# Attention over 16 batches on one core: x transposed by TensorE in every body, the projection's bias written by VectorE, other buffer rings

## The reference

```python
qkv = (x @ w_qkv).reshape(b, n, 3, H, hd).transpose(2, 0, 3, 1, 4)
q, k, v = (qkv[0], qkv[1], qkv[2])
attn = jnp.einsum('bhnd,bhmd->bhnm', q, k) * scale
attn = jnp.where(attn_mask[None, None] == 0, -jnp.inf, attn)
attn = jax.nn.softmax(attn, axis=-1)
o = jnp.einsum('bhnm,bhmd->bhnd', attn, v).transpose(0, 2, 1, 3).reshape(b, n, d)
o = o @ w_proj + b_proj
...
return o + ln                      # ln: layer norm of o, with gamma and beta
...
x = _layernorm(x + _L0_gnn_ref(x, ...), axis=-1)
```

## Time and profile before

| | |
|---|---|
| median of 3 runs | 3227.46 us (3222.18 to 3236.81) |
| the profiled execution | 3231.68 us, of which the span is 3229.8 us |
| PE busy | 2994.3 us, 93% of the span |
| POOL, ACT, DVE busy | 2628.1, 2624.1, 2197.0 us |
| mean granted clock of PE | 0.973 of full speed |

### The profile page before, as it was taken

One profiled execution on the slowest core, in us unless ns is written; L12 is line 12 of the kernel. 1 busy time (PEld: TensorE's weight loads), 2 busy tenths in 40 slices (PEclk: granted clock), 3 DMA queues, 4 the chain that ended last, 5 costly groups with the idle time before them and its releaser, 6 DMA issues.

```text
span 3229.8 us, 119607 instructions
## 1 busy us (share of the span) xinstructions
PE 2994.3 (93%) x42112; PEld 1842.0 (57%) x42112; DVE 2197.0 (68%) x4243; ACT 2624.1 (81%) x3790; POOL 2628.1 (81%) x1610
## 2 busy tenths in 40 slices
PE   5889999899998999999999998999999899999995
PEld 2556556565565556656566565556556566565562
DVE  4546667677676767767677676767767677676775
ACT  5878878788787878878788787888888788787882
POOL 4768878788787878878798797888878788787884
PEclk9989999999999999999999999999999999999997
DMA  8999999999999999999999999999999999999994
GB/s 225 192 199 195 211 214 218 218 208 220 211 212 218 215 214 219 216 212 219 214 216 214 215 213 222 216 215 220 216 214 219 212 212 219 212 215 218 216 208 108
DMA packets 2320778, 682.49 MB, mean 211 GB/s; under 512 B 2268498, under 2 KB 2268498, under 8 KB 2320724
## 3 DMA queue, kind: packets, MB, share of 16 engines
q1 hardware_dynamic: 2266724, 581.58, 97.3%
q10 hardware_dynamic: 54000, 100.16, 9.7%
HBM read 77.60 MB, written 33.55 MB: 34 GB/s over the span
## 4 chain that ended last, share of the span: by engine, by line
POOL 54%; issue 29%; SPq 7%; PE 6%; DMA 2%; DVE 1%; POOLq 1%; ACT 1%; ACTq 0%; DVEq 0%
POOL p_split L742 42%; SPq L307 5%; POOL x_res L758 4%; POOL x_split L776 4%; POOL norm L766 2%; POOL norm L761 2%; PE scores_a L401 1%; PE side L360 1%; SPq L285 1%; DMA pt<-p_split 1%; PE side L347 1%; POOL shift L769 1%; POOLq L741 1%; PE proj L383 0%; PE pv_bank L422 0%
## 5 line engine op out<-in xcount | busy, mean ns | idle before, releaser
L742 POOL TENSOR_TENSOR p_split<-p,p_split 128x1024 f16<-128x1024 f32 x1024 | 2172.4, 2138 | 531.8 <-ACT p_split L507 526.0
L494 ACT ACTIVATE p<-p,row_min 128x1024 f32<-128x1024 f32 x1024 | 1167.9, 1142 | 91.9 <-DVE row_min L638 89.8
L507 ACT ACTIVATE p_split<-p 128x1024 f16<-128x1024 f32 x1024 | 1053.6, 1046 | 206.8 <-DMA pt<-p_split 205.9
L638 DVE CUSTOM_DVE_ANT_0 p<-scores_a,mask_q 128x1024 f32<-128x1024 f32 x512 | 626.9, 1224 | 502.3 <-PE scores_b L401 481.9
L422 PE MATMUL pv_bank<-v_both,pt 128*128 128x64 f16 x8192 | 840.0, 195 | 26.5 <-DMA pt<-p_split 24.6
L424 PE MATMUL pv_bank<-v_both,pt 128*128 128x64 f16 x8192 | 840.6, 195 | 0.0
L423 PE MATMUL pv_bank<-v_both,pt 128*128 128x64 f16 x8192 | 840.5, 195 | 0.0
L422 PEld LDWEIGHTS pv_bank<-v_both,pt 128*128 128x128 f16 x8192 | 747.9, 99 | 115.2 <-issue 39.6
L360 PE MATMUL side<-xt,w_hi 128*128 128x512 f16 x2048 | 683.2, 391 | 119.3 <-DMA xt<-x_split 114.3
L423 PEld LDWEIGHTS pv_bank<-v_both,pt 128*128 128x128 f16 x8192 | 736.9, 99 | 84.4 <-issue 6.0
L424 PEld LDWEIGHTS pv_bank<-v_both,pt 128*128 128x128 f16 x8192 | 737.4, 99 | 0.0
(11 more groups left out here) (80 smaller groups left out, 4261.3 us busy)
## 6 DMA issues: line engine op xcount, KB each, us to landing
x_in<-in_x ACTq DMA_DIRECT2D x63, 512.0 KB, 5.1
x_res<-in_x ACTq DMA_DIRECT2D x120, 256.0 KB, 3.3
out<-x_res ACTq DMA_DIRECT2D x120, 256.0 KB, 3.7
pt<-p_split SPq DMA_TRANSPOSE x1024, 4.8
pt<-in_adj SPq DMA_DIRECT2D x8, 512.0 KB, 9.7
ot<-in_L_gnn_w_qkv SPq DMA_DIRECT2D x4, 768.0 KB, 9.8
p<-in_x SPq DMA_DIRECT2D x4, 512.0 KB, 5.3
p<-in_x ACTq DMA_DIRECT2D x8, 256.0 KB, 8.5
```

The source lines that it names most:

```text
L494: nc.scalar.activation(p32[:, slot, :], p32[:, slot, :], ACT.Exp, bias=row_min[:, slot:slot + 1], scale=-1.0, accum_out=row_sum[:, head:he ...
L507: nc.scalar.activation(p_split[:, head % RING, HI, :], p32[:, head % RING, :], ACT.Copy).then_inc(hi_done, 1)
L638: nc.vector.tensor_tensor_reduce(out=p32[:, slot, :], in0=scores[ab][:, :], in1=mask_q[:, u, :], scale=-SCALE, scalar=3.0e38, op0=ALU.add, ...
L742: nc.gpsimd.tensor_tensor(p_split[:, slot, LO, :], p32[:, slot, :], p_split[:, slot, HI, :], ALU.subtract).then_inc(lo_done, 1)
```

## The change

X becomes a side item. `X0` and `X1` are four float32 transposes each by PE of the two tiles in `x_in`, into a side bank; ACT takes the high part into `xt` and DVE the low one, as it takes any other side item. This happens in every body but the last batch's, so `xt` is held twice, addressed by the batch's parity, and `x_split`, the DMA transposes of x and the splits of x on ACT and POOL are gone, with the waits of Q0 and K1 for them. The first batch's x is transposed the same way ahead of body -1. The bias is written by DVE: after each last read of the projection's bank a `seed` puts 256 times the bias into it, and the twelve products accumulate on it; P0 and P1 have twelve items, the `ones` product is gone, and P waits for its seed where it waited for the last read. `p_split` becomes a ring of eight (`SPLIT`), `pt` one of four (`TURNED`). The loop covers bodies 5 to 58. Slots of takes move: Q1 is taken at slots 3 and 4.

```diff
 RING = 4
-TURNED = 8
+TURNED = 4
+SPLIT = 8
...
-ORDER = [("Q1", 0, 12), ("V0", 0, 48), ("V1", 0, 48), ("P0", 0, 4), ("O1", 0, 4), ("P0", 4, 13), ("Q0", 0, 12),
-         ("K0", 0, 12), ("K1", 0, 12), ("P1", 0, 9), ("O0", 0, 4), ("P1", 9, 13)]
+ORDER = [("Q1", 0, 12), ("X0", 0, 4), ("V0", 0, 48), ("V1", 0, 48), ("P0", 0, 4), ("O1", 0, 4), ("P0", 4, 7),
+         ("X1", 0, 4), ("P0", 7, 12), ("Q0", 0, 12), ("K0", 0, 12), ("K1", 0, 12), ("P1", 0, 9), ("O0", 0, 4),
+         ("P1", 9, 12)]
...
-LOOP = (PAIRS + 1, GROUPS - 1)
+LOOP = (PAIRS + 1, GROUPS - PAIRS - 1)
...
-TAKE_DVE = {"Q1": 6, "V0": 10, "V1": 12, "O1": 14, "Q0": 22, "K0": 29, "K1": 29, "O0": 30}
+TAKE_DVE = {"Q1": 4, "X0": 5, "V0": 10, "V1": 11, "O1": 14, "X1": 15, "Q0": 22, "K0": 29, "K1": 30, "O0": 30}
...
-        x_split = sb("x_split", [P, T // 2, 2, 2, D], F16)
-        xt = sb("xt", [P, T, 2, KC, P], F16)
+        xt = sb("xt", [P, 2, T, 2, KC, P], F16)
...
-                for u in range(UNITS):
-                    for p in range(T // 2):
-                        if u == XT_UNIT[p] and not (known(g) and g == FIRST_GROUP):
-                            transposing(sp, g, lambda: turn_x(g, p))
...
+                elif kind[0] == "X":
+                    if i == 0 and half == 0:
+                        wait_alone(pe, x_in_loaded, g * 16 + 16)
+                    mm = nc.tensor.transpose(bank[:, i * P:(i + 1) * P], x_in[:, half, i * P:(i + 1) * P], ident[:, :])
...
-                    mm = nc.tensor.matmul(bank[:, c * P:(c + 1) * P], xt[:, t, rows, k, :], w[:, k, OF_V, pair(g), :],
+                    mm = nc.tensor.matmul(bank[:, c * P:(c + 1) * P], xt[:, parity(batch(g)), t, rows, k, :],
+                                          w[:, k, OF_V, pair(g), :],
                                           start=(i == 0), stop=(i % 12 == 11), skip_group_check=True)
...
-                    if i == 0 and kind == NEXT_FIRST:
-                        wait_alone(pe, x_turned[0], batch(g + 1) * 32 + 32)
-                    if i == 0 and kind == "K1":
-                        wait_alone(pe, x_turned[1], batch(g + 1) * 32 + 32)
+                    if i == 0 and kind == NEXT_FIRST and active(g, "X1"):
+                        wait_alone(pe, side_dve, side_done(g, "X1"))
...
-                else:
-                    nc.tensor.matmul(proj_bank(g, half), ones[:, :], bias_rows[:, :], start=False, stop=True).then_inc(proj_ready, 1)
...
+                elif kind[0] == "X":
+                    nc.scalar.activation(xt[:, parity(batch(g + PAIRS)), pair(g) * 2 + half, HI, :, :],
+                                         bank[:, :].rearrange("p (k n) -> p k n", k=KC), ACT.Copy).then_inc(side_act, 1)
...
-                before = unit_before(ug, uk, RING // 2)
+                before = unit_before(ug, uk, SPLIT // 2)
                 if not known(before[0]) or before[0] >= 0:
-                    wait(act, turned[(head - RING) % TURNED], turned_before(before[0], before[1], ab) + 16)
+                    wait(act, turned[(head - SPLIT) % TURNED], turned_before(before[0], before[1], ab) + 16)
...
+            def seed(g, i):
+
+                nc.vector.tensor_scalar(proj_bank(g, i), bias_b[:, :], WSCALE, None, ALU.mult).then_inc(seeds(g, i)[0], 1)
...
                     nc.vector.scalar_tensor_tensor(xr, bank, norm[:, i:i + 1], xr, ALU.mult, ALU.add).then_inc(summed, 1)
+                    wait_alone(dve, summed, n + 1)
+                    if not known(g) or g < GROUPS - 1:
+                        seed(g + i, 1 - i)
...
-            def split(g):
-                if known(g) and not 0 <= batch(g) < B - 1:
-                    return
-                wait_alone(pool, x_hi_done, g + PAIRS + 1)
-                nc.gpsimd.tensor_tensor(x_split[:, pair(g), :, LO, :], x_in[:, :, :], x_split[:, pair(g), :, HI, :],
-                                        ALU.subtract).then_inc(x_lo_done, 1)
```

More of the change, by code:

```diff
@@ L233, in bodies @@
                 body(g)
-        def transposing(eng, g, do):
-            if not known(g):
-                with eng.If((g & 3) == 3):
-                    do()
-            elif (g + 1) % PAIRS == 0 and 0 <= batch(g + 1) < B:
-                do()
         def heads(g, u, ab):
@@ L257, in proj_bank, with seeds @@
             return scores[0][:, 0:CH] if known(g) and g >= GROUPS and i == 1 else proj[:, :]
+        def seeds(g, i):
+            if known(g) and g >= GROUPS:
+                return (seeded[0], projected(GROUPS, 0) + (g - GROUPS + 1)) if i == 0 else (seeded[1], g - GROUPS + 1)
+            return seeded[0], projected(g, i) + 1
         def last_tile(g, i):
@@ L272, in _ @@
         def _(sp):
-            for t in range(T // 2):
-                sp.dma_start(x_first[:, t, :, :], x_pairs[t, :, :, :]).then_inc(x_first_loaded[t], 16)
+            for t in range(T):
+                sp.dma_start(x_first[:, t, :], x_tiles[t, :, :]).then_inc(x_first_loaded[t], 16)
             for kc in range(KC):
@@ L327, in _, with first_turn @@
             pe.wait_ge(ident_ready, 1)
+            def first_turn(t):
+                pe.wait_ge(x_first_loaded[t], 16)
+                wait(pe, x_first_lo, t - 1)
+                for k in range(KC):
+                    mm = nc.tensor.transpose(side[t % 2][:, k * P:(k + 1) * P], x_first[:, t, k * P:(k + 1) * P], ident[:, :])
+                mm.then_inc(x_first_turned, 1)
             def side_matmul(g, kind, i):
@@ L370, in project @@
                         pe.wait_ge(w_ready, 4 * KC)
-                        pe.wait_ge(bias_ready, 4)
-                    if known(g) and g >= GROUPS:
-                        pe.wait_ge(min_done, heads(GROUPS, 0, 0))
-                        pe.wait_ge(summed, projected(g, half) - (1 if g > GROUPS or half else 0))
-                    else:
-                        wait_alone(pe, summed, projected(g, half))
+                    wait_alone(pe, *seeds(g, half))
                     if half == 0:
@@ L425, in times_v @@
                 mm.then_inc(pv_done, 1)
+            for t in range(T):
+                first_turn(t)
+            for k in range(KC):
+                mm = nc.tensor.matmul(proj[:, k * P:(k + 1) * P], ident[:, :], ident[:, :], start=(k == 0), stop=True,
+                                      skip_group_check=True)
+            mm.then_inc(bits_set, 1)
             def body(g):
@@ L619, in take @@
                                             ot[:, HI, parity(batch(og)), pair(og), tiles, :], ALU.subtract).then_inc(side_dve, 1)
+                elif kind[0] == "X":
+                    at, tile = parity(batch(g + PAIRS)), pair(g) * 2 + half
+                    nc.vector.tensor_tensor(xt[:, at, tile, LO, :, :], bank[:, :].rearrange("p (k n) -> p k n", k=KC),
+                                            xt[:, at, tile, HI, :, :], ALU.subtract).then_inc(side_dve, 1)
                 elif kind[0] == "V":
@@ L715, in body @@
                     if known(g) and g == FIRST_GROUP and s == 0:
-                        prepare_weights()
+                        for t in range(T):
+                            first_low(t)
+                            if t % 2:
+                                prepare_weights(t // 2)
                         for t in range(T):
```

152 lines of the change are left out of this document (64 added, 88 removed).

## The result

The changed kernel takes 3246.1 us (median of 7 runs, 3243.4 to 3253.8), the kernel before in the same series 3229.9; the ratio is 1.005, with a 95% interval from 1.0038 to 1.0061. It is slower by a half per cent, where a gain of one per cent was forecast; the time lies inside the wide range of 3130 to 3250, at its upper end. The profiled execution took 3243.4 us, its span 3241.6.

What follows compares the result with a forecast made beforehand. PE, busy 93% of the span, bounds the kernel. Loop body 46.06 - 0.29 - 0.43 + 0.93 + 2.1, taken as 48.35; the bodies' -29.5 with start and end makes -31.5, median 3196 us, range 3130 to 3250.

Steps and rivals of the forecast that it cites:

- the term for register instructions and the lost lead: V in loop bodies: 1.3 us for register instructions plus 0.7 for the lost lead, 2.0 in replay, 2.1 in the sum.
- V0's wait for Q1's low part: Ahead of V0: ends 1.1 to 1.5 us into unit 1's products, nearly spends the sequencer's lead, costs 0.7 us.
- the transposes: X0 and X1 on PE: eight at a step of 0.12 us add 0.93 us a body.
- Break-even: Loop body at which the total would not change: 48.93 us.
- Rival (b): V0's wait ends later than 1.9 us into unit 1, lead spent throughout; body 49.5, total 3258; chance 0.13.
- The stall for x: Long bodies, ahead of Q0: the whole excess of 9.2 us goes, 15 x 9.2 = 139 us.
- The bias: Two bias products a body leave PE: -0.43 us.
- O0's gap: Transposes of O0 waiting for K0's low part: the gap of 0.3 us in a short body goes, -0.29.
- rival (d): TURNED = 4 or X's takes delay times_v by 0.5 to 0.8 us a body: 3223 to 3239; chance 0.1.
- rival (c): Transposes of x cost their printed length or slow the clock: +1.3 us a body, 3274; chance 0.03.
- Rival (a): V's register instructions hide as their printed length says: loop body 46.3 to 46.5, total 3091; chance 0.11.
- being written out: Bodies outside the loop have fixed addresses: 46.3 us each, four of them behind the loop.

Runs made afterwards that it cites:

- before_reg: The kernel before with V's tile of xt in the loop indexed by a register that always holds zero: 3279.7 us, ratio 1.0155.
- x_after_v: The changed kernel with X0 moved from ahead of V0 to behind O1, so V0 doesn't wait for Q1's low part: 3414.5 us, ratio 1.0568.
- rings_old: The changed kernel with the old rings, four heads of split probabilities and eight of transposed ones: 3246.2 us, ratio 1.0044.
- x_first: The changed kernel with X0 ahead of Q1, so V0 waits for X0's take instead: 3213.4 us, ratio 0.9940.
- x_first63: x_first with the loop to body 62, no wait of Q0 for X1, and second-tile scaling two slots later: 3195.9 us, ratio 0.9898.
- mix_late: x_first63 with 24 V0 products dealt among Q1's last four and X0 taken a slot earlier on ACT: 3178.7 us, ratio 0.9832.
- branch: x_first without Q0's wait for X1, and units 1 and 2 written twice on PE behind a branch on batch parity: 3824.8 us, ratio 1.1833.
- loop8: The changed kernel with eight bodies in the loop, run six times, making pair and parity constants: 3365.0 us, ratio 1.0417.
- xv: x_first without Q0's wait, scaling two slots later, V reading a third x copy filled by DMA each batch, four-head rings: 3276.7 us, ratio 1.0140.

## Why the prediction was wrong

**The step that failed** is the size of the term for register instructions and the lost lead: 2.1 us a body in the sum, of which 1.3 for the instructions by themselves and 0.7 for V0's wait for Q1's low part. The failing part is the 0.7. The table gives the term as V's growth, 2.31, the transposes' excess over 0.93, 0.43, and what P has above 6.49 - 0.43 - 0.29 = 5.77, 0.09: together 2.83. The same is left of 49.10 with the other terms as forecast: 49.10 - 45.34 - 0.93 = 2.83. The 0.73 above the forecast are 40 us in 54 bodies, which turned a gain of one per cent into a loss of a half. Break-even, 48.93, was right.

**Why it was mis-sized.** The mechanism stands. Register instructions alone cost 1.39 in `before_reg`, where 1.3 was worked out. What is left for the wait is 2.83 - 1.39 = 1.44, and `x_after_v`, where V0 doesn't wait for Q1, has 1.2 to 1.4 less in V and the transposes. So the wait cost about twice its 0.7. The wait ended 1.6 us into unit 1, not 1.1 to 1.5, so that PE stood some 0.35 us ahead of V0, and no lead was left for V's first eleven products. They took 1.78 us, 0.62 before. There three register instructions belong to three products, for w's addresses are made there too, 0.39 us and not 0.25; in `before_reg` the same instructions for w run while the array is busy with Q1's last products and the scores, and its first 16 V products take 1.04 us. The prediction priced two instructions to three products everywhere.

Rival (b), with a chance of 0.13, is the nearest of the five, but not what happened as it was put: V runs at the sequencer's pace from its first product, as it said, and the body passed its 48.95, yet the wait ended before the 1.9 us that it asked for, the gap ahead of V0 was below its 0.5, and the body was 49.10 and not 49.5. That its total (3258) is near 3246 is in part chance. It should have had a chance near that of the forecast, since my reading of the wait's end was within 0.4 us of its threshold.

**What was right.** The stall for x went, all of it, and all bodies of the loop have one length; the granted clock was 1.00 in the body from 1457.68 to 1506.78 (the earlier trace rows had 0.94 in a long body). The bias left P: 6.49 less O0's gap of 0.29 is 6.20, which less 0.43 is 5.77; P is at 5.86, with a new gap of 0.23 ahead of Q0 in it, where Q0 waits for X1's take. (The gap of 0.46 ahead of P0 is in V's sum.) O0's gap went. The rings cost 0.11 us a body at most (`rings_old`), so rival (d), which had 0.5 to 0.8, falls. A transpose of x costs 0.12 from start to start where nothing holds it (0.96 for eight in `x_first`), so rival (c) falls. The Trainium skill, "TensorE: Matmul & The Clock Gate", Part 4, gives some 275 ns for a transpose in a kernel's context: the printed length agrees (0.28 in the earlier trace rows), the price in a row does not. What it says of the clock, no run here tests, since the transposes are 1 us of a body of 49. Rival (a) falls with `before_reg`: the printed 32 and 46 ns are not the price of a register instruction. The interval between their starts, 0.11 to 0.13 us, is. The Trainium skill, "Perfetto Trace Analysis", "Sequencer-only Instruction", leaves fetch and decode out of the printed time of such an instruction; the distance of 0.11 beside the printed 32 and 46 ns agrees.

**The smaller terms.** First scores came 6.5 us earlier than before (39.26 against 45.72), not 3. Entering the loop cost 2 us, not 7. The first five bodies took 2 less. Against that, the four bodies that the change had put outside the loop took 46.6, 50.0, 47.8 and 50.3 us, 9.5 more than four of 46.3, with PE waiting for head DMAs; being written out was costed at nothing. The end took 4.3 more, not 1. Set against what was forecast for each, all these came to some +3 together.

**What stays open.** That instruction loads slow the transposes is shown as a coincidence in four kernels, the changed one the first of them (0.98 MB and 4.9 us; 5.90 MB and 5.8; 9.68 MB and 5.8; `x_first63` with 0.62 MB and no slow tail), not by a run that loads instructions and does nothing else. How much of the 0.80 us that V lost in `mix_late` is the dealing and how much the earlier take was not separated. No kernel has V0's wait over well before V0 and no other wait beside it, so what V costs with register instructions and its full lead in the changed kernel's order is known only from V's sum in `x_after_v`. Seeding by DVE alone was not tried in the kernel before, for lack of room in SBUF.

## What to carry to other kernels

Before an operand's address is made to depend on a loop variable, count the register instructions that the inner products get and compare their pace (0.11 us each here) with the array's: short products (0.056 us) can't hide them, long ones (0.22 us) can. Dealing the two kinds among each other, with the take a slot earlier, gave back 0.35 us a body here. A wait that ends just as its work is due is not free even if it shows no gap, since it stops the sequencer and takes away the lead that hides everything else. Constant addresses bought with more code or more DMA traffic cost more here than they gave: head DMAs already took SP 40 of 46 us, and with a branch in the loop PE stood at it.

## What the runs showed of the hardware that I had not expected

- In `branch`, where PE passes over a stretch of its code and its loop is longer by two units, PE stood twice a body, 493.5 us in 107 pieces, 4.6 us each in the mean. In `loop8` it stood 4.6 us at each of five new turns of a loop of eight bodies. The changed kernel's loop of one body (664 products and 217 instructions of the sequencer a turn) goes back with no gap.
- Transposing DMAs were slower beside a little other traffic: in the run with 5.9 MB of instruction loads in 3360 us they take 5.8 us instead of 4.9, and with a copy of 2 MB each batch four bodies took 6 to 13 us longer than four of 46.76 (`xv`).
- Added work on a resource can be free where a stall absorbs it: 1.39 us more in each body of `before_reg` cost nothing in the 15 bodies that waited for x.
